# Attention's row maxima in two sets for the first batch, and scores that begin at half the chunks

## What is computed

```
q, k, v = (heads(x @ w) for w in (wq, wk, wv))      # 16 heads of 16 channels
q, k = apply_rope(q, k, sin, cos)                   # layer 0
att = softmax(q @ k.T / sqrt(16))                   # layer 0
att = softmax(q @ k.T / sqrt(16) + alibi + causal)  # layer 1
y = (att @ v) merged over the heads, @ wo
```

## Time and profile before

| | us |
|---|---|
| median of 3 runs | 2843.71 |
| lowest, highest | 2838.93, 2847.15 |
| profiled execution, its own time | 2837.38 |
| its span in the trace | 2835.6 |
| PE busy | 2615.9 (92%) |
| DVE busy | 1945.1 (69%) |
| ACT busy | 1269.8 (45%) |
| first attention: first chunk, first score | 240.89, 289.46 |
| second attention: first chunk, first score | 1780.41, 1813.18 |

### The profile page before, as it was taken

How to read it: one execution, slowest core, us unless ns; L and a number is a source line. 1 busy time by engine, 2 the same in 40 slices (tenths; PEclk the granted TensorE clock), 3 DMA queues, 4 the chain that set the end, 5 groups by cost and what they waited for, 6 DMA issues and landing times. The chain is left out here.

```text
span 2835.6 us, 38818 instructions
## 1 busy us (share of the span) xinstructions
PE 2615.9 (92%) x14164; PEld 1255.9 (44%) x14164; DVE 1945.1 (69%) x4168; ACT 1269.8 (45%) x1936; POOL 655.7 (23%) x640
## 2 busy tenths in 40 slices
PE   5888999999999999787898997999999999898998
PEld 3442333333333332344555654454445554555665
DVE  6968878778787885685774335777667675576334
ACT  3431566566566667443212322355455556321221
POOL 1544223232141200253002440212121110001441
PEclk9996999999999999998999999799999999999999
DMA  3003330321303400002202654633134330301565
GB/s 122 1 17 89 51 62 18 57 47 28 57 24 51 62 1 2 1 1 80 80 34 67 153 118 121 98 69 61 42 53 68 63 57 2 112 34 34 126 161 157
DMA packets 162593, 175.78 MB, mean 62 GB/s; under 512 B 19090, under 2 KB 135762, under 8 KB 162258
## 3 DMA queue, kind: packets, MB, share of 16 engines
q1 hardware_dynamic: 146948, 152.57, 24.8%
q0 software_dynamic: 12416, 17.84, 3.8%
q10 hardware_dynamic: 3040, 2.88, 0.4%
HBM read 116.32 MB, written 56.13 MB: 61 GB/s over the span
## 5 line engine op out<-in xcount | busy, mean ns | idle before, releaser
L1820 DVE TENSOR_REDUCE a_mx<-a_bank 128x1 f32<-128x512 f32 (+3 forms) x1792 | 1036.6, 627 | 263.2 <-PE a_bank L1554 183.1
L1690 ACT ACTIVATE a_E<-a_bank 128x1024 f32<-128x1024 f32 (+3 forms) x896 | 796.1, 931 | 459.4 <-PE a_bank L1611 313.4
L1554 PE MATMUL a_bank<-a_KT,a_QT 96*128 96x512 bf16 (+4 forms) x1792 | 593.7, 376 | 25.3 <-DVE a_mx L1820 16.2
L1611 PE MATMUL a_bank<-a_QT,a_KT 99*128 99x512 bf16 (+4 forms) x1792 | 509.1, 359 | 4.2 <-DMA a_QT<-a_mT 2.3
L1626 PE MATMUL a_bank<-a_E,a_Vg 128*32 128x512 f32 (+3 forms) x3584 | 437.7, 560 | 0.7 <-ACT a_E L1690 0.7
L1554 PEld LDWEIGHTS a_bank<-a_KT,a_QT 96*128 96x128 bf16 (+1 forms) x1792 | 151.9, 98 | 514.4 <-DVE a_mx L1820 323.5
L1611 PEld LDWEIGHTS a_bank<-a_QT,a_KT 99*128 99x128 bf16 (+1 forms) x1792 | 170.7, 99 | 175.9 <-ACT a_E L1690 30.9
L983 ACT ACTIVATE d_silu<-d_bank 128x512 f32<-128x512 f32 x96 | 57.2, 596 | 367.6 <-PE d_bank L857 367.6
L872 PE MATMUL d_bank<-wdT,d_hT 128*128 128x256 f32 (+1 forms) x768 | 198.4, 402 | 4.2 <-DVE d_hT L1072 4.2
L433 POOL TENSOR_TENSOR f_hl<-f_hT,f_hh 128x512 f16<-128x512 f32 x96 | 111.9, 1166 | 353.2 <-ACT f_hh L450 351.3
L776 POOL DMA_INDIRECT d_xg<-normalised,d_index x64 | 67.5, 1054 | 518.2 <-issue 516.7
(11 more groups left out here) (239 smaller groups left out, 3521.8 us busy)
## 6 DMA issues: line engine op xcount, KB each, us to landing
parts<-a_parts SPq DMA_DIRECT2D x64, 384.0 KB, 2.6
a_QT<-parts SPq DMA_DIRECT2D x180, 128.0 KB, 5.8
a_KT<-parts SPq DMA_DIRECT2D x180, 128.0 KB, 9.0
d_wgu<-in_L_ffn_w_gate SPq DMA_DIRECT2D x64, 176.0 KB
d_wgu<-in_L_ffn_w_up SPq DMA_DIRECT2D x64, 176.0 KB
d_wd<-in_L_ffn_w_down SPq DMA_DIRECT2D x64, 176.0 KB
normalised<-d_xn SPq DMA_DIRECT2D x8, 1152.0 KB, 4.7
acc<-d_zero SPq DMA_DIRECT2D x2, 4224.0 KB, 15.5
```

The costliest lines, as they stand in the source:

```text
L1554: last = nc.tensor.matmul(out[:, 0:w], QT[0:W, h, qt * P:(qt + 1) * P], KT[0:W, h, kh * HALF:kh * HALF + w], start=True, stop=not diag)
L1611: last = nc.tensor.matmul(out, KT[:, h, kt * P:(kt + 1) * P], QT[:, h, half * HALF + c0:(half + 1) * HALF], start=True, stop=not diag)
L1690: nc.scalar.activation(E[:, u % 2, 2 * pair:2 * pair + 2, c0:HALF], bank[:, 2 * pair:2 * pair + 2, c0:HALF], ACT.Exp).then_inc(exps, 1)
L1820: nc.vector.tensor_reduce(mx[:, x[1] // C % 2, j, qt, kh:kh + 1], out[:, 0:w], AX.X, ALU.max).then_inc(freed_dve, 1)
```

## The change

The groups of the first batch (G = 0 to 3) get their row maxima in two sets, one for each half of the queries; later groups keep one. `row_sets` lists the sets, numbered k: 8 of two halves, then 12 whole ones, 20 in each attention where there were 16. Set 0 is complete after C0 chunks, which is 32 in the first attention and 16 in the second. The opening now issues FIRST chunks, 52 and 48, in place of 80 and 68, with `turn_m` of set 0 three chunks behind its last chunk; each unit then issues 4 and 5 chunks by turns (`9 * n // 2`) until the stream has its former lead again, after 56 units in the first attention and 40 in the second. From there on the two orders are the same. A set is measured in the unit in which its last chunk has been issued (`m_unit[k]`), turned two units later, and the scores wait for its rows where that half of the queries begins (`at_unit`). On SP, `rows(0)` stands behind `write(0, 5)` and not behind `write(0, 7)`. `mparts` is flat and cleared once. The diff, with one line of context:

```diff
@@ -1284,3 +1284,22 @@
     AHEAD = (5 if second else 4) * C // U
-    m_unit = next(u for u in range(U) if AHEAD + C * u // U >= C)
+    U0 = sum(1 for h, _, _ in units if h == 0)
+    C0 = C * U0 // U if second else C // 2
+    FIRST = C0 + (32 if second else 20)
+
+    def issued(n):
+
+        return min(FIRST + 9 * n // 2, C + AHEAD + C * n // U)
+
+    row_sets = [(G, h) for G in range(BG) for h in ((0, 1) if G < NG else (None,))]
+    at_unit = {(G, u): row_sets.index((G, h)) for G, h in row_sets for u in (U0 if h else 0,)}
+
+    def complete(k):
+
+        G, h = row_sets[k]
+        return G * C + (C0 if h == 0 else C)
+
+    m_unit = [next(n for n in range(BG * U) if issued(n) >= complete(k)) if k else -1 for k in range(len(row_sets))]
+    for k, (G, h) in enumerate(row_sets):
+        assert k == 0 or m_unit[k] + 3 < G * U + (U0 if h else 0), (k, m_unit[k])
+    measured = {m_unit[k]: k for k in range(1, len(row_sets))}
     y_unit = 2 + next(u for u in range(U) if units[u][0])
@@ -1293,3 +1312,3 @@
                      + [("value", 0, n) for n in range(4)])
-    opening = ahead_of_rows + some(0, C + 3) + [("turn_m", 0)] + some(C + 3, C + AHEAD)
+    opening = ahead_of_rows + some(0, C0 + 3) + [("turn_m", 0)] + some(C0 + 3, FIRST)
     closing = [("turn_y", BG - 1, 1)] + [(kind, B - 1, n) for kind, n in
@@ -1303,3 +1322,3 @@
 
-    beside = {(n // U, n % U): some(C + AHEAD + C * n // U, C + AHEAD + C * (n + 1) // U) for n in range(BG * U)}
+    beside = {(n // U, n % U): some(issued(n), issued(n + 1)) for n in range(BG * U)}
     for G in range(BG):
@@ -1320,5 +1339,6 @@
         beside[G, y_unit].insert(0, ("turn_y", G, 0))
-        if G + 1 < BG:
-            beside[G, m_unit + 2].insert(0, ("turn_m", G + 1))
-        else:
+        for u in range(U):
+            if G * U + u - 2 in measured:
+                beside[G, u].insert(0, ("turn_m", measured[G * U + u - 2]))
+        if G + 1 == BG:
             for u, kind, k in ((1, "turn_o", 0), (2, "turn_o", 1), (3, "out", 0), (4, "out", 1)):
@@ -1357,3 +1377,3 @@
         mrest = sb(tag + "mrest", [P, GH, TPB])
-        mparts = sb(tag + "mparts", [P, GH, 3, TPB], BF16)
+        mparts = sb(tag + "mparts", [P, GH * 3 * TPB], BF16)
         mT = sb(tag + "mT", [GH * 3 * TPB, P], BF16)
@@ -1446,8 +1466,14 @@
 
-                def rows(G):
+                def rows(k):
 
-                    sp.wait_ge(freed_dve, freed_at(("turn_m", G)))
+                    G, h = row_sets[k]
+                    sp.wait_ge(freed_dve, freed_at(("turn_m", k)))
                     for j in range(GH):
-                        dst = QT[W:WM, G % NG * GH + j, :].rearrange("r (q c) -> r q c", c=P)
-                        sp.dma_start(dst, mT[j * 3 * TPB:(j + 1) * 3 * TPB, :]).then_inc(m_rows, 16)
+                        if h is None:
+                            dst = QT[W:WM, G % NG * GH + j, :].rearrange("r (q c) -> r q c", c=P)
+                            src = mT[j * 3 * TPB:(j + 1) * 3 * TPB, :]
+                        else:
+                            dst = QT[W:WM, G % NG * GH + j, h * HALF:(h + 1) * HALF].rearrange("r (q c) -> r q c", c=P)
+                            src = mT[(h * GH + j) * 3 * KPH:(h * GH + j + 1) * 3 * KPH, :]
+                        sp.dma_start(dst, src).then_inc(m_rows, 16)
 
@@ -1461,8 +1487,10 @@
                 load(0, 1)
-                for n in range(4, NJ):
-                    write(0, n)
+                write(0, 4)
+                write(0, 5)
                 rows(0)
+                write(0, 6)
+                write(0, 7)
                 load(0, 2)
                 load(0, 3)
-                todo = [(G * U + m_unit + 2, rows, (G + 1,)) for G in range(BG - 1)]
+                todo = [(m_unit[k] + 2, rows, (k,)) for k in range(1, len(row_sets))]
                 for b in range(1, B):
@@ -1473,3 +1501,3 @@
                         G, u = unit_of("proj", b, 3 if g < 2 else 7)
-                        todo.append((max(G * U + u + 5, ((b - 1) * NG + g + 1) * U, G * U + m_unit + 3), load, (b, g)))
+                        todo.append((max(G * U + u + 5, ((b - 1) * NG + g + 1) * U, G * U + 14 * U // 16), load, (b, g)))
                 for _, step, which in sorted(todo, key=lambda x: x[0]):
@@ -1560,3 +1588,3 @@
                         last = nc.tensor.transpose(out[0:GH * 3 * TPB].bitcast(BF16)[:, 0:P],
-                                                   mparts[:].rearrange("p j r q -> p (j r q)"), ident_b[:])
+                                                   mparts[:], ident_b[:])
                     elif kind == "turn_y":
@@ -1636,4 +1664,5 @@
                 for G in range(BG):
-                    pe.wait_ge(m_rows, START + (G + 1) * GH * 16)
                     for u in range(U):
+                        if (G, u) in at_unit:
+                            pe.wait_ge(m_rows, START + (at_unit[G, u] + 1) * GH * 16)
                         score_pair(G, u, 0)
@@ -1792,20 +1821,25 @@
 
-                def maxima(G, step):
+                def maxima(k, step):
 
+                    G, h = row_sets[k]
+                    own = slice(0, TPB) if h is None else slice(h * KPH, (h + 1) * KPH)
+                    n = TPB if h is None else KPH
+                    lo = GH * 3 * KPH if h else 0
+                    part = mparts[:, lo:lo + GH * 3 * n].rearrange("p (j r q) -> p j r q", j=GH, r=3)
                     if step == 0:
-                        dve.wait_ge(freed_dve, freed_at(("chunk", (G + 1) * C - 1)))
-                        if G:
-                            dve.wait_ge(filled, START + place["turn_m", G - 1] + 1)
-                        nc.vector.tensor_reduce(m[:], mx[:, G % 2], AX.X, ALU.max).then_inc(m_step, 1)
+                        dve.wait_ge(freed_dve, freed_at(("chunk", complete(k) - 1)))
+                        if k:
+                            dve.wait_ge(filled, START + place["turn_m", k - 1] + 1)
+                        nc.vector.tensor_reduce(m[:, :, own], mx[:, G % 2, :, own, :], AX.X, ALU.max).then_inc(m_step, 1)
                         return
-                    dve.wait_ge(m_step, START + G * 5 + step)
+                    dve.wait_ge(m_step, START + k * 5 + step)
                     if step == 1:
-                        nc.vector.tensor_scalar(mparts[:, :, 0, :], m[:], -1.0, None, ALU.mult).then_inc(m_step, 1)
+                        nc.vector.tensor_scalar(part[:, :, 0, :], m[:, :, own], -1.0, None, ALU.mult).then_inc(m_step, 1)
                     elif step == 2:
-                        nc.vector.scalar_tensor_tensor(out=mrest[:], in0=m[:], scalar=-1.0, in1=mparts[:, :, 0, :],
+                        nc.vector.scalar_tensor_tensor(out=mrest[:, :, own], in0=m[:, :, own], scalar=-1.0, in1=part[:, :, 0, :],
                                                        op0=ALU.mult, op1=ALU.subtract).then_inc(m_step, 1)
                     elif step == 3:
-                        nc.vector.tensor_copy(mparts[:, :, 1, :], mrest[:]).then_inc(m_step, 1)
+                        nc.vector.tensor_copy(part[:, :, 1, :], mrest[:, :, own]).then_inc(m_step, 1)
                     else:
-                        nc.vector.tensor_tensor(mparts[:, :, 2, :], mrest[:], mparts[:, :, 1, :], ALU.subtract).then_inc(m_step, 1)
+                        nc.vector.tensor_tensor(part[:, :, 2, :], mrest[:, :, own], part[:, :, 1, :], ALU.subtract).then_inc(m_step, 1)
 
@@ -1859,2 +1893,3 @@
                     normalise(0, i)
+                nc.vector.memset(mparts[:], 0.0)
                 if second:
@@ -1887,3 +1922,3 @@
                     take(x)
-                    if x == ("chunk", C - 1):
+                    if x == ("chunk", C0 - 1):
                         for step in range(5):
@@ -1897,5 +1932,6 @@
                     for u in range(U):
-                        step = 0 if u == m_unit and G + 1 < BG else 5
-                        if step == 0:
-                            maxima(G + 1, 0)
+                        k = measured.get(G * U + u)
+                        step = 0 if k else 5
+                        if k:
+                            maxima(k, 0)
                         if g == 0 and u < 4 and b + 1 < B:
@@ -1907,6 +1943,6 @@
                                 step += 1
-                                maxima(G + 1, step)
+                                maxima(k, step)
                         while step < 4:
                             step += 1
-                            maxima(G + 1, step)
+                            maxima(k, step)
                         for x in beside[G, u - 1] if u else beside[G - 1, U - 1] if G else ():
```

## The result

The changed kernel takes 2853.42 us (median of 12 runs, 2850.09 to 2860.88) against 2844.69 of the kernel before in the same session (12 runs, 2838.80 to 2849.90). The ratio is 1.0041, with a 95% interval of 1.0031 to 1.0051: 11.7 us more, 8.8 to 14.5; the two medians differ by 8.7. That is slower by just over the 0.3% that I had set as the bound. I had given "no change" 0.60 and "slower" 0.22; the time lies within the range, 5 us above the forecast.

A forecast was written before the change was run, and what follows sets the result against it. The prediction took DVE to bound the openings and PE everything from the first score on. Its terms, -26.1 + 6.2 + 3.3 + 0.5 + 0.5 + 20.2, gave +4.6 us, a median of 2848.3 us, range 2832 to 2860.

The forecast's parts named there:

- no change: Whole kernel: measured time within 0.3%, 8.5 us, of the kernel before; chance 0.60.
- slower: Whole kernel: measured time more than 0.3% above the kernel before; chance 0.22.
- the wait for rows: Scores wait a second time inside groups 0 to 3, mainly at unit 4 of the second attention: +0.5 us, bounds 0 and 3.
- the largest one, DVE's: Groups 0 to 3: half of DVE's 40.3 us of work other than reductions falls on PE, +20.2 us.
- The openings: Before each attention's first score: 28 chunks fewer save 16.7 us, 20 fewer save 9.4 us; together -26.1 us.
- the third rival: Set steps, groups 0 to 3: each waits out POOL on the shared port; sum +12.8 us, 2856.5 us, chance 0.06.
- The chunks on PE: Moved chunks return in the first 56 and 40 units: +6.2 and +3.3 us, plus 0.5 for eight more turns.
- the second rival: First batch: DVE becomes the bound, nearly all its other work falls on PE; whole bill +24.7 us, 2868.4, chance 0.13.
- the fourth rival: First scores: set 0's rows arrive late, half of the 26.1 us is lost; sum +17.6 us, 2861.3, chance 0.03.
- PE alone sets the pace: Groups 0 to 3: DVE keeps up, so they grow only 6 and 4 us; sum -15.6 us, 2828.1, chance 0.18.

The follow-up runs named there:

- second experiment: Kernel before, with two sets per group of the first batch in the first attention only, old opening and pace kept: 2840.19 us, ratio 0.9997.
- The first experiment: Changed kernel, but in the second attention SP issues the rows of group 0's second half between load(0, 2) and load(0, 3): 2847.68 us, ratio 1.0019.

## Why the prediction was off, point by point

The time fell into the range, and the sum was 4 to 7 us too low. One term was missed by 7.6 us, the wait for rows. That the largest one, DVE's, came out right is luck, since both of its factors were wrong.

**The openings** came as said: -15.7 for -16.7 and -9.2 for -9.4, with first scores at 32.9 and 23.6 us (31 to 33 and 23 to 25 were named). The missing microsecond is set 0's steps: 2.1 us beside POOL for 1.1 before. The Trainium skill (SBUF — State Buffer, Who interferes with whom) says that a DVE instruction in a two-port mode or with two SBUF inputs and a GpSimd instruction block each other for the whole of the earlier one. The 0.98 agrees: the step began at 261.54, while a POOL instruction was under way from 261.34 to 262.49, and ended 0.03 us after it. This blocking didn't make the third rival: with the steps in the body of the attention the sets cost 0.4 us (second experiment).

**The chunks on PE** were not measured by themselves; 6.2 and 3.3 stand as a floor, and the 9.6 us that are left with the shortest reductions are consistent with 6.2.

**DVE.** The term was right, its factors weren't. It isn't measured by itself: it is what the windows leave when PE's own share is taken off, 10.7 us in the first attention, of which 6.9 are seen as waits and 3.2 stay with the shortest reductions; in the second, with the rows mended, it is 164.4 - 152.2 = 12.2 less 3.3 and 0.25, 8.7. That is 19.4 for the predicted 20.2. But I had put it down to DVE's other work, 40.3 us with half of it falling on PE. The other work is 16.2 + 13.2 = 29.4: a set costs DVE 0.4 to 0.5 us more, not 1.8. The share, if all of it is counted as this work, is 19.4 of 29.4, 66%, above the 60% from which I had said the second rival would win, yet of a smaller bill. So the forecast of 20.2 was met by a bill that was too large and a share that was too small. Three widths of reduction show that most of it hangs on DVE's time per chunk (17.1, 11.9, 9.6), and two comparisons put the part of the burst behind P times V at 2.8 to 4.5 of it. That a backlog is carried from unit to unit, as the second rival has it, was not shown.

**The wait for rows is the step that failed.** I took 0.5 us, bounds 0 and 3; it was 4.84 of waiting and some 8.1 with the slower clock behind it. I had set "5.4 to 6 against 5.4", and the 5.4 came from group 4, where the queue was empty. For the second set of the second attention I didn't ask what stands ahead of it on that queue: two more loads of 12 transfers each, which `rows(1)` is issued behind. I did name the mechanism in the fourth rival, "behind SP's writes or in the DMA queue", but for set 0 only, where the margin was five microseconds. The first experiment shows it: the rows between the loads, and the 8.1 us are gone. The turn and the issues came as reckoned; by them alone the wait would have been 0.3 us.

**The sum again**, with what was measured: -24.9 (openings) + 6.2 + 3.3 + 0.5 + 19.4 + 8.1 = +12.6, and with the 0.8 of groups 4 to 15, which is noise, the 13.3 of the two attentions but for rounding, against 11.7 timed. It must come out so, since the DVE term is what the others leave. With the rows at 0.5 it is +5.0, beside the forecast of +4.6. Of the rivals, "PE alone sets the pace" (+6 and +4 for the groups) is excluded by 17.1 and 12.2.

**Left open**: 3.2 us of the first attention's 17.1, which are there even with reductions of 0.33, and the opening that is 1.8 us longer when the rows go between the loads. A fourth bank, and steps of set 0 that don't meet POOL, weren't tried. **The better kernels** are the one before with a third item ahead of P times V (0.9934), the change with that and the rows mended (0.9921), and the change in the first attention alone with it (0.9935). Their intervals overlap; the first is the least edit.

## What to carry to other kernels

Starting sooner only pays if the moved work costs less where it lands. Here a chunk cost 0.60 us in the opening, since DVE sets the pace there, and came back at 17.1 / 28 = 0.61 in the first attention, though PE itself needs 0.22: its tightest neighbour, DVE, had little room left in a unit, and PE waited for it. Before a small transfer is given a deadline, count the bytes that stand ahead of it on its queue at that place; a latency read where the queue was empty says nothing of it. And where an engine works in bursts against few buffers, try moving one item out of the burst first: one line was worth more than the whole rearrangement.

## What the runs showed that I had not expected

- Four DMAs of rows (3 KB each) behind 24 loads of 128 KB on one queue arrived 5.8 us after their last issue, against 1.3 with the queue empty.
- One stall of 4.84 us in a stretch where PE is otherwise nearly full was followed by 6.8 us at a granted clock of 0.50. The stall and what followed cost some 8 us together. It is no accident of one run: with the third item in all units the same place has a stall of 6.3 us, with short reductions 5.5, with half reductions 6.3, and with the third item in units of five chunks 5.0.
- DVE's short steps took 0.98 and 0.47 us beside POOL's split in the opening, 0.47, 1.01 and 0.52 in another run, where 0.16 to 0.18 is the median. The steps that make the parts were hit (L1837 and L1842 in the profile above), the reduction L1833 not (0.19, and never above 0.22 in 40 executions).
- With one more item ahead of P times V the whole kernel is 0.7% faster, though PE's share of busy time was 92% before. Its modelled busy time fell by 6.1 us in groups 4 to 15 of the first attention (628.96 to 622.83), with the same instructions.
